# Quantised attention in a decoder kernel: no extra barriers ahead of it, v's bias by halves, maxima and results turned between later scores, and its output computed by batch in the next stage

## The reference, cut to what matters

```python
x = x + L1_attn(layernorm(x));  x = x + L1_xattn(layernorm(x), ctx);  x = x + L1_ffn(layernorm(x))

def L1_attn(x):                                # 16 heads of width 8
    qkv = fake_quant(x, axis=-1) @ fake_quant(qkv_w, axis=0).T + qkv_b
    q, k, v = split into heads
    attn = softmax(fake_quant(q) @ fake_quant(k).T / sqrt(8))
    out = attn @ fake_quant(v)
    return fake_quant(out) @ fake_quant(proj_w, axis=0).T + proj_b
```

## Time and profile before

| | us |
|---|---|
| median of 3 runs | 698.66 |
| lowest and highest | 698.02, 702.86 |
| the profiled execution | 694.07 |
| its span | 692.3 |
| mean granted clock of TensorE, of full speed | 0.924 |
| busy: PE, DVE, ACT, POOL | 581.7, 418.8, 383.8, 94.7 |

### The profile page before, as it was taken

The page is one execution under the profiler, slowest core; times in us unless marked ns, Lnnn a source line. Parts: engine busy times, 40 slices in busy tenths (PEclk is TensorE's granted clock), DMA queues, the critical chain, the costliest instruction groups (busy, mean ns, idle before and its releaser), DMA issues. The chain is left out here.

```text
span 692.3 us, 9379 instructions
## 1 busy us (share of the span) xinstructions
PE 581.7 (84%) x3281; PEld 316.5 (46%) x3281; DVE 418.8 (60%) x859; ACT 383.8 (55%) x682; POOL 94.7 (14%) x99
## 2 busy tenths in 40 slices
PE   2379899989999687999999996389888857977978
PEld 1112233322333544889998984011222145445756
DVE  8268577567731744645653236878998076537664
ACT  2246867667666356657564430357898713774611
POOL 7200200100001003600000000597000000003000
PEclk9759999999999998999999996568999889997999
DMA  5324200543071502000000000000000002000000
GB/s 157 91 37 57 73 21 2 70 64 52 2 305 26 66 1 94 27 1 1 1 1 3 13 0 1 0 1 1 2 2 2 0 1 94 6 1 0 1 17 15
DMA packets 14785, 22.68 MB, mean 33 GB/s; under 512 B 3524, under 2 KB 9908, under 8 KB 14356
## 3 DMA queue, kind: packets, MB, share of 16 engines
q1 hardware_dynamic: 12916, 15.54, 11.3%
q10 hardware_dynamic: 1824, 6.55, 2.5%
HBM read 9.99 MB, written 0.52 MB: 15 GB/s over the span
## 5 line engine op out<-in xcount | busy, mean ns | idle before, releaser
L536 DVE TENSOR_REDUCE negmax<-ps 128x2 f32<-128x1024 f32 x96 | 113.9, 1221 | 41.0 <-PE ps L467 40.5
L583 ACT ACTIVATE probs<-ps 128x512 f32<-128x512 f32 x192 | 105.9, 598 | 38.6 <-PE ps L486 36.7
L583 ACT ACTIVATE probs_q<-ps,score_scale 128x512 f32<-128x512 f32 x128 | 78.1, 687 | 14.7 <-PE ps L486 13.1
L1857 PEld LDWEIGHTS ps<-experts,hid 128*128 128x128 f32 x640 | 82.7, 191 | 6.9 <-issue 1.0
L1857 PE MATMUL ps<-experts,hid 128*128 128x128 f32 x640 | 84.0, 275 | 0.0
L536 DVE TENSOR_REDUCE negmax_q<-ps 128x2 f32<-128x1024 f32 x64 | 74.7, 1219 | 6.1 <-PE ps L467 5.6
L1934 ACT ACTIVATE hid<-ps 128x512 f32<-128x512 f32 x80 | 47.0, 598 | 48.0 <-PE ps L864 47.9
L864 PE MATMUL ps<-experts,wfc 128*128 128x512 f32 x156 | 49.3, 424 | 0.0
L467 PE MATMUL ps<-gated 64*128 64x512 bf16 x128 | 29.2, 428 | 20.3 <-DMA gated<-parts 9.2
L2028 DVE SCALAR_TENSOR_TENSOR x_tok<-ps,comb,x_tok 128x128 f32<-128x128 f32 x64 | 18.0, 344 | 43.2 <-PE ps L1857 43.2
L500 PE MATMUL ps<-probs_q,v_q 128*32 128x512 f32 x256 | 43.3, 674 | 0.0
(11 more groups left out here) (382 smaller groups left out, 939.7 us busy)
## 6 DMA issues: line engine op xcount, KB each, us to landing
q_wide<-parts SPq DMA_DIRECT2D x12, 256.0 KB, 5.7
k_wide<-parts SPq DMA_DIRECT2D x12, 256.0 KB, 7.0
experts<-in_L_ffn_Wfc_dram ACTq DMA_DIRECT2D x1, 2560.0 KB, 9.5
experts<-in_L_ffn_Wproj_dram ACTq DMA_DIRECT2D x1, 2560.0 KB, 15.8
gated<-parts SPq DMA_DIRECT2D x18, 128.0 KB, 2.4
qs_x<-crossing SPq DMA_DIRECT2D x5, 256.0 KB, 3.0
w<-in_L_ffn_W_dram SPq DMA_DIRECT2D x1, 1024.0 KB, 5.3
square_weights<-in_squares_dram SPq DMA_DIRECT2D x1, 768.0 KB, 7.1
```

Source lines behind the costliest of these rows:

```text
L536: nc.vector.tensor_reduce(maxima, scores, AX.X, ALU.max, negate=True).then_inc(self.a_max_done, 1)
L583: nc.scalar.activation(self.probs[0:size, g % self.P_SLOTS, :], ps[0:size, self.B_BANK + g % self.B_SLOTS, :], ACT.Exp, scale=scale).then_ ...
L1857: last = nc.tensor.matmul(K.ps[:, y_bank(g), i * P:(i + 1) * P], hid[:, m % SLOTS, i * P:(i + 1) * P], wproj[:, FT * e + f, :], start=(f = ...
```

## The change

1. `recycle` is gone. `release` only clears semaphores, with no barrier. The first block's are cleared when the experts' block begins, those two blocks' when the quantised attention begins, each time on GpSimd behind the barrier in which every block ends.
2. v's bias is written by halves: half 0 at the end of `experts_gelu`, once ACT has copied `h_ft` of half 1's layer norm (`h_ready`), half 1 at the start of the quantised attention.
3. The extremes of q and v are reduced per half (512 columns), k's still over both. One small reduction joins q's and v's halves.
4. `QuantAttention` has `T_LAG` 5 and `M_LAG` 2: from unit 16 on, M is written 2 units later than it would be, and T 5 units behind E instead of 4.
5. Everything behind the last result moves into the next block, as `QuantOutputs`: scaling and rounding half by half, projection half by half, and the layer norm of half 0 between the two additions to x. PE projects q of half 0 before it turns half 1.

```diff
-    def recycle(self, keep=()):
-
-        done = [n for n in self.made if n not in keep]
-        self.nc.all_engine_barrier()
-        self.nc.clear_and_free_semaphores([self.made.pop(n) for n in done])
-        self.nc.all_engine_barrier()
+    def release(self, names):
+
+        self.nc.clear_and_free_semaphores([self.made.pop(n) for n in names])
...
+                if self.M_LAG is not None and n >= 16:
+                    late += [(g + self.M_LAG, ("M", w, 0)) for w in turn + whole]
+                    turn, whole = [], []
                 order += [("M", w, 0) for w in turn]
...
             next_ln.turn(pe, 1)
+            pe.wait_ge(next_ln.h_ready, 1)
+            Q.bias_of_values(K, 0)
...
     lead_growth = 4
+    T_LAG, M_LAG = 5, 2
...
+    def ints(self, dve, b):
+        nc, n = self.K.nc, self.n
+        tiles = self.tok_a[:, b * TPB:(b + 1) * TPB, :]
+        self.range.scaled(nc.vector, tiles, tiles).then_inc(n["o_scaled"], 1)
+        dve.wait_ge(n["o_scaled"], b + 1)
+        self.range.ints(nc.vector, self.o_ints[:, b * TPB:(b + 1) * TPB, :], tiles).then_inc(n["o_ints"], 1)
...
+    def ends_by_half(dve, a, done):
+        for b in range(NB):
+            dve.wait_ge(done, b + 1)
+            product = K.ps[:, BANK[a] + b, :]
+            chain(nc.vector.tensor_reduce(half_ends[:, 0, a, b:b + 1], product, AX.X, ALU.min, negate=True))
+            chain(nc.vector.tensor_reduce(half_ends[:, 1, a, b:b + 1], product, AX.X, ALU.max))
...
         def _(pe):
-            for b in range(NB):
-                nc.tensor.matmul(K.ps[:, BANK[2] + b, :], Q.ones_row[0:1, 0:P],
-                                 Q.bias[0:1, 2, :].unsqueeze(1).broadcast_to([1, TPB, D]), start=True, stop=False,
-                                 skip_group_check=True)
+            Q.bias_of_values(K, 1)
             pe.wait_ge(n["w_high"], 1)
...
-            for a in range(3):
-                dve.wait_ge((n["q_done"], n["k_done"], n["v_done"])[a], 2)
-                last = qkv_range.reduce(chain, K.ps[:, BANK[a]:BANK[a] + 2, :].rearrange("p b t -> p (b t)"), a)
-                if a < 2:
-                    chain(last)
-            last.then_inc(spread_qkv.reduced, 1)
+            ends_by_half(dve, 0, n["q_done"])
+            dve.wait_ge(n["k_done"], 2)
+            chain(qkv_range.reduce(chain, K.ps[:, BANK[1]:BANK[1] + 2, :].rearrange("p b t -> p (b t)"), 1))
+            ends_by_half(dve, 2, n["v_done"])
+            nc.vector.tensor_reduce(qkv_range.tile[:, 0:2, 0:3:2], half_ends[:, :, 0:3:2, :], AX.X, ALU.max) \
+                .then_inc(spread_qkv.reduced, 1)
...
         @block.tensor
         def _(pe):
+            outputs.spread_range(pe)
             keep_busy(K, 6, 6)
-            ln.tensor(pe)
             for b in range(NB):
+                outputs.turn(pe, b)
+            keep_busy(K, 6, 1)
+            for b in range(NB):
+                outputs.project(pe, b)
+            keep_busy(K, 6, 6)
+            for b in range(NB):
+                ln.turn(pe, b)
                 ln.wait_half(pe, b)
...
         @block.scalar
         def _(act):
-            ln.scalar(act)
+            ln.table(act)
+            outputs.out_first(act)
+            ln.std(act, 0)
+            ln.evacuate(act, 0)
+            ln.std(act, 1)
...
         @block.vector
         def _(dve):
-            ln.vector(dve)
+            outputs.find_range(dve)
             for b in range(NB):
-                low_part(dve, b)
+                outputs.ints(dve, b)
+            outputs.out_second(dve)
+            outputs.add(dve, 0)
+            ln.stats(dve, 0)
+            outputs.add(dve, 1)
+            ln.normalise(dve, 0)
+            ln.stats(dve, 1)
+            ln.normalise(dve, 1)
+            low_part(dve, 0)
+            dve.wait_ge(ln.turned, NT)
+            nc.vector.tensor_copy(K.h_ft[:, HALF:2 * HALF], K.ps[:, ln.banks[1], :]).then_inc(ln.h_by_dve, 1)
+            low_part(dve, 1)
             att.vector(dve)
```

120 lines of the change are left out of this document (69 added, 51 removed).

## The result

The changed kernel took 702.18 us in the median of 20 runs (696.56 to 713.66), the kernel before 695.93 in 20 runs beside them. The ratio is 1.0071, 95% interval [1.0045, 1.0096]: slower by 0.7%, where 687.0 was forecast and the range ended at 693.5. The profiled execution took 702.63, its span is 700.9. Medians are over all executions; ratios and their intervals leave out those that took over 1.5% longer than the fastest of the same kernel.

What follows compares the result with a forecast made beforehand. No engine was full in the attention: waits between PE, ACT and DVE bound it, and chains of small steps its ends. Gains of 2.5 + 7.4 + 1.8 = 11.7 us gave 687.0, range 682.5 to 693.5.

Steps and rivals of the forecast that it cites:

- The rival that decided: Attention: TensorE falls to 1.2 GHz, 16 us a period; from three periods of five on slower than before, 703; chance 0.05.
- Term 1: Hand-over into the quantised attention: fewer barriers and v's bias by halves start q's matmuls earlier; gain 2.5 us, bounds 1.3 to 3.3.
- The join: Hand-over: the small DVE operation that joins the halves' extremes, 12 numbers per partition into 4, would take 0.2 us.
- Term 2: Quantised attention: the new order of T and M gains 7.4 us over start-up, steady periods and end; bounds 0.5 and 9.7.
- The steady part: Five attention periods: each falls from 11.41 to 10.65 us with DVE as the bound; gain 3.8 us.
- Both waits have cover: Steady periods: ACT's wait for M and DVE's for the cast are covered by a B and an A.
- the waits move: Steady periods: ACT lags, so DVE still waits for the cast of the maxima; the 3.8 us are lost, 690.8; chance 0.2.
- The start-up: Attention ahead of the steady periods: M's wait and one A come back on DVE; gain 2.0 us, bounds 0 and 3.3.
- The end: Behind the last A step: a B between V and T shortens ACT's standstill; gain 1.6 us, bounds 0.5 and 2.17.
- Term 3: Output, from the attention's results to the cross-attention's first score: work by halves gains 1.8 us, bounds 0.5 and 2.4.
- The sum: Whole kernel: the gains at the hand-over, attention and output add to 11.7 us, ending at 687.0.
- The late maxima: Attention jobs: the remainder waits out a DVE reduction, so the maxima's DMA is late; 2.4 us lost, 689.4; chance 0.1.

Runs made afterwards that it cites:

- experiment 11: Changed kernel with k's two reductions made three times on DVE, so the attention begins 5.0 us later: 708.25 us, ratio 1.0193.
- experiment 6: Changed kernel with only M moved (M_LAG 2, T 4 units behind E as before): 693.57 us, ratio 0.9991.
- 2: Kernel before with the attention's new order alone (T_LAG 5, M_LAG 2): 703.63 us, ratio 1.0080.
- 4: Changed kernel measured again, unchanged: 702.56 us, ratio 1.0102.
- 5: Changed kernel with only T moved (T_LAG 5, M where it was): 700.13 us, ratio 1.0056.
- 1: Changed kernel with the attention's old order (without T_LAG 5, M_LAG 2): 696.54 us, ratio 0.9977.
- 7: Changed kernel, old order, one unread matmul behind every second B step once the last maxima are turned: 693.20 us, ratio 0.9966.
- 9: Changed kernel with only M moved, M given its own PSUM bank and B left with two: 704.92 us, ratio 1.0156.
- 12: Changed kernel, old order, k's two reductions made three times so the attention begins 5.0 us later: 704.19 us median of 4, ratio 1.0117.
- 14: Changed kernel, old order, unread matmuls behind M and T and behind every second B step at the end: 699.16 us, ratio 1.0022.
- 18: Second measurement of the kernel before with the hand-over's edits and unread matmuls behind every second B step at the end: 694.17 us, ratio 0.9969.
- 15: Changed kernel with old order and old hand-over, leaving only the output by batch: 697.14 us, ratio 1.0016.
- experiment 10: Changed kernel, old order, unread matmuls at the attention's end and also at its start: 716.29 us median.
- 3: Changed kernel (new order) with unread matmuls, two behind each M and one behind each T: 693.73 us, ratio 0.9969.
- 8: Changed kernel (new order) with unread matmuls behind M and T and behind every second B step at the end: 694.24 us, ratio 0.9985.
- 13: Changed kernel (new order), unread matmuls behind M and T, attention begun 5.0 us later: 697.94 us, ratio 1.0039.
- 17: Kernel before with the hand-over's edits and unread matmuls behind every second B step at the end: 692.61 us, ratio 0.9963.
- 16: Kernel before with the hand-over's edits alone (old order, old output): 699.07 us median, ratio 0.9998.

## Why the prediction was wrong, point by point

**The rival that decided** was the clock, which had a chance of 0.05. Its price was right, 16 us for a period at 1.2 GHz, measured 16.3 in the changed kernel and up to 17.3 in experiment 11. But the condition "at least three periods of five" was wrong: one period and the last 24 exponentials were enough, +5.22 and +4.85 us, because the forecast's gains in the steady part weren't there to be used up first. That its 703 is so near the measured 702.2 is luck. The step that failed is "Against it: the clock stays at 1.00 with PE busy 10.04 of 11.41, and that share rises". The share did not rise, since the period got no shorter (10.17 of 11.54, 0.88 both times), and the clock fell; in experiment 6 it was 9.83 of 11.98 and the clock stayed. The busy share of a period is no forecast of the clock. The Trainium skill, "TensorE: Matmul & The Clock Gate", section "A second HAM failure mode: psum-queue depth-cycling", tells of PE pausing between groups of matmuls as it goes round its PSUM banks, and of a clock that goes up and down by it. That page would have raised the rival's chance. This trace agrees with it only in part: the fall comes behind waits of 0.23 and 0.46 us, one of them for a PSUM pair, but the same two waits at the three hand-overs before it brought no fall.

What sets it off is T's place, as far as these traces tell. All five with T late and no fillers (after, 2, 4, 5, 11) are at 1.2 GHz for 13 to 38 us of the five periods. Of the twelve with T where it was, eleven (before, 1, 6, 7, 9, 12, 14 to 18) have nothing of it but the end of a dip of 3.4 us at the first hand-over (before and 15); the twelfth, experiment 10, has 66 us of it, in the longest of its executions. The three with T late and fillers (3, 8, 13) have none. Experiments 5 and 6 part T from M, also by their times (all 12 executions of 5 at 697.4 or more, nine of 12 of 6 at 694.2 or less). Experiment 2 shows that the order alone is enough, and 3 and 13 that work for PE at the hand-over prevented it in both places in time. Which hand-over it is isn't settled by the order alone: in 2 and 4 it is the one that begins the fifth period, in 5 the one that begins the first, and in 11, the changed kernel begun 5 us later, also the first. Why T's place does it, while M's longer waits don't, was not settled: PE's waits were not varied by themselves.

**Term 1, the hand-over, 2.5 us**: right, measured 3.18 - 0.21 = 2.97. The first q matmul came 3.18 earlier, not 2.65: half 0's bias began at 418.51 - 1.51 = 417.00, counted as in the trace of before, where I had put it at 417.75. It didn't wait for the copy of half 1, as the rows of the result show. The join took 0.16 for a forecast of 0.2, and what follows gave back 0.21 for 0.15. The gain is that of the barriers and the bias. By the earlier trace rows whole reductions would take 9.62 us from the first q matmul to their end, and the halves took 433.08 + 0.16 - 423.40 = 9.84; so the halves bought nothing by this estimate, and no run has the one without the other.

**Term 2, the attention, 7.4 us**: wrong, apart from the clock too. With the clock held (experiment 3) its parts are:
- The steady part, 3.8: a loss of 0.9 (57.97 against 57.08), some of it the fillers'. The step that failed is "Both waits have cover". M and the A step behind it stand in the same two pairs, so DVE waits for that A as long as it had waited for the cast (2.5 us in four periods, before 3.4 in five). The rival "the waits move" named the right outcome by the wrong way: it is not ACT that lags but the pair that isn't free. Experiment 9 shows the wait gone with a bank for M, at the price of one of B's.
- The start-up, 2.0: measured 1.9 (28.02 to 26.12 in 3 and in 6), and most of it comes back as a wait behind the boundary. Both stretches together won 1.0, where 5.8 was forecast.
- The end, 1.6: not shown. At full clock the last 24 took 15.25 in experiment 11 and 16.13 in 13, against 16.93 before at a clock of 0.85, which is 0.8 to 1.7 less. But no run has the old order at full clock there without a filler (with one, 17.35), so what of this is the order's and what the clock's stays open. In the changed kernel they ran mostly at 1.2 GHz.

**Term 3, the output, 1.8 us**: wrong in size, and it had no part in the time. Three pairs of runs differ by the output alone. From the last exponential to the first score it took 26.47 in 15 against 26.98 before, 25.41 in 7 against 26.03 in 17, and 27.81 in 1 against 27.47 in 16: gains of 0.5 and 0.6, and a loss of 0.3. The two additions to x and half 0's low part in 7, where the last exponential ends at 548.40:

```profile
563.00 0.75 DVE L2282 SCALAR_TENSOR_TENSOR x_tok<-ps,out_range,x_tok 128x512 f32<-128x512 f32 x1 [1.62 <-PE ps L2246]
...
570.02 0.75 DVE L2639 SCALAR_TENSOR_TENSOR crossing<-ps,columns_by_strip,crossing 128x512 fp32r<-128x512 f32 x1
```

And in 17, where it ends at 550.78:

```profile
564.00 1.58 DVE L2393 SCALAR_TENSOR_TENSOR x_tok<-ps,out_range,x_tok 128x512 f32<-128x512 f32 x2 [0.98 <-PE ps L2299]
...
573.00 0.75 DVE L2613 SCALAR_TENSOR_TENSOR crossing<-ps,columns_by_strip,crossing 128x512 fp32r<-128x512 f32 x1 [1.08 <-ACT crossing L2645]
```

The layer norm by halves did what was forecast: 7.02 us from the first addition to half 0's low part instead of 9.00 (forecast 7.10). The step that failed is "the first addition starts at about 565.85 instead of 565.80". In 7 it came 14.60 us behind the last exponential instead of 13.22, in 15 it came 15.62 behind it instead of 14.17, so 1.4 later. Half 1's rounding, for which PE waits before it projects half 0, ends 0.5 later, 0.3 of it the barrier's, and the projection ran at 1.2 GHz in 7 and 15. Where it ran at full clock (13) the addition came 13.60 behind, 0.4 later, but then the projection of q for half 1 was at 1.2 GHz, as in the changed kernel. Alone (15) the output gained nothing at the end.

**The sum** took it for granted that a gain at its place is a gain at the end. Behind the first score of the cross-attention the same code takes 113.6 to 118.1 us in the twenty traces, and this goes with the granted clock over it: 113.6 to 114.9 where it is 0.93 or 0.94, 116.2 at 0.91 (10), 117.5 to 118.1 at 0.90. In 16, which begins this part with the 3 us of the hand-over in hand, it is 0.90 for 0.94 before, and the 4.1 us that it costs take back more than the gain. That the earlier start is what brings the fall is argued: the start was not varied with all else the same. The late maxima, the other rival, did not come: no wait for their DMA stands in the list of the four periods.
